# Second norm and norm statistics moved inside a chunk of a Mamba block with a quantised linear layer

## The reference

```
x = x + mamba(layernorm(x))
x = x + layernorm(x) @ W.T + bias          # W = scale * (code - 128), 1024 x 1024, blocks of 32

mamba(u): x1, z = split(u @ in_proj)       # 1024 -> 2 x 2048
          xc  = silu(conv4(x1) + conv_b)   # causal convolution over rows
          dt_r, B, C = rmsnorm(xc @ x_proj.T, ...)         # 64, 16, 16 columns
          dt  = softplus(dt_r @ dt_proj.T + dt_bias)
          h_t = exp(dt_t * A) * h_(t-1) + dt_t * B_t * xc_t    # 2048 channels x 16 states
          y   = (sum_n C_t h_t + D * xc) * silu(z)
          return y @ out_proj.T            # 2048 -> 1024
```

## Time and profile before

| | |
|---|---|
| median of 3 runs | 4703.04 us (4701.97 to 4705.4) |
| profiled execution | 4697.21 us |
| its span, first to last instruction | 4695.4 us |
| mean granted TensorE clock (1 = full) | 0.972 |
| busy: PE matmul, PE weight load | 4448.9 us (95%), 4049.0 us (86%) |
| busy: VectorE, GpSimd, ScalarE | 4160.0 us (89%), 4039.2 us (86%), 3542.4 us (75%) |

### The profile page before, as it was taken

One profiled execution on the slowest core, in us unless ns is written; L12 is line 12 of the kernel. 1 busy time (PEld: TensorE's weight loads), 2 busy tenths in 40 slices (PEclk: granted clock), 3 DMA queues, 4 the chain that ended last, 5 costly groups with the idle time before them and its releaser, 6 DMA issues.

```text
span 4695.4 us, 80181 instructions
## 1 busy us (share of the span) xinstructions
PE 4448.9 (95%) x26656; PEld 4049.0 (86%) x26656; DVE 4160.0 (89%) x5745; ACT 3542.4 (75%) x8848; POOL 4039.2 (86%) x2942
## 2 busy tenths in 40 slices
PE   7788989999999999999999999999999999999889
PEld 6567879989898998989989898998989889898779
DVE  3898989989899998989989899998989989899981
ACT  3777787877778787777877878787787777778760
POOL 0898989989898998989989898998989899899990
PEclk9889999999999999999999999999999999999999
DMA  7324243353434435343353534334353443434232
GB/s 255 130 79 161 99 159 139 114 186 133 173 129 161 145 138 175 124 178 128 123 188 123 177 137 165 137 128 173 138 180 120 145 165 129 165 127 155 90 115 94
DMA packets 160285, 678.56 MB, mean 145 GB/s; under 512 B 21120, under 2 KB 30080, under 8 KB 110720
## 3 DMA queue, kind: packets, MB, share of 16 engines
q1 hardware_dynamic: 141440, 639.88, 39.0%
q10 hardware_dynamic: 18432, 33.56, 1.9%
HBM read 618.32 MB, written 55.05 MB: 143 GB/s over the span
## 4 chain that ended last, share of the span: by engine, by line
PE 59%; DVE 20%; POOL 7%; issue 6%; ACT 5%; DMA 1%; SPq 0%; DVEq 0%; POOLq 0%; ACTq 0%
PE g L767 13%; PE gx L594 13%; PE ys L574 12%; DVE hb L1342 11%; PE ys L614 9%; PE g L689 4%; POOL dbx L486 4%; DVE hc L1290 4%; DVE gx L1238 2%; POOL half L494 2%; PE ys L604 2%; DVE bst L1218 2%; PE gx L581 2%; ACT hb L1061 1%; PE hb L853 1%
## 5 line engine op out<-in xcount | busy, mean ns | idle before, releaser
L1342 DVE TENSOR_TENSOR_SCAN hb<-hb,dbx 128x512 f32<-128x512 f32 x2048 | 2498.0, 1220 | 108.0 <-ACT hb L1061 84.4
L486 POOL TENSOR_TENSOR dbx<-dtx,bb 128x1024 f32<-128x1024 f32 x1024 | 2421.0, 2364 | 60.1 <-DVE hb L1342 34.9
L1061 ACT ACTIVATE hb<-dt,a_neg 128x256 f32<-128x256 f32 x4096 | 1789.5, 468 | 66.3
L494 POOL TENSOR_TENSOR half<-hc 128x512 f32<-128x512 f32 x1024 | 1303.1, 1273 | 135.4 <-DVE hc L1290 120.4
L1290 DVE TENSOR_TENSOR hc<-hb,cb 128x512 f32<-128x512 f32 x2048 | 1378.9, 673 | 0.0
L574 PE MATMUL ys<-half,ident 128*128 128x256 f32 x4096 | 1073.2, 389 | 133.4 <-POOL half L494 119.2
L574 PEld LDWEIGHTS ys<-half,ident 128*128 128x128 f32 x4096 | 757.2, 194 | 254.3 <-POOL half L494 151.3
L767 PEld LDWEIGHTS g<-wo,ybuf 128*128 128x128 f32 x7680 | 954.0, 198 | 20.2 <-issue 1.3
L767 PE MATMUL g<-wo,ybuf 128*128 128x128 f32 x7680 | 966.7, 281 | 0.6 <-issue 0.6
L614 PE MATMUL ys<-xnT,wz 128*128 128x256 f32 x4096 | 928.8, 380 | 1.6 <-DVE ybuf L1301 1.6
L594 PE MATMUL gx<-xnT,wx 128*128 128x256 f32 x3968 | 904.5, 381 | 4.3 <-DMA wx<-in_win 2.6
(11 more groups left out here) (105 smaller groups left out, 2766.1 us busy)
## 6 DMA issues: line engine op xcount, KB each, us to landing
wz<-in_win SPq DMA_DIRECT2D x128, 1024.0 KB, 4.8
wx<-in_win SPq DMA_DIRECT2D x124, 1024.0 KB, 4.8
wo<-in_wout SPq DMA_DIRECT2D x123, 1024.0 KB, 4.9
wf<-wf_scratch SPq DMA_DIRECT2D x113, 512.0 KB, 3.2
xc_scratch<-xcn ACTq DMA_DIRECT2D x128, 256.0 KB, 2.1
xcs<-xc_scratch SPq DMA_DIRECT2D x128, 256.0 KB, 5.0
bb<-bc_scratch SPq DMA_DIRECT2D x64, 512.0 KB, 7.5
cb<-bc_scratch SPq DMA_DIRECT2D x64, 512.0 KB, 6.7
```

The costliest lines, as they stand in the source:

```text
L486: nc.gpsimd.tensor_tensor(dbx[:, k % 2, :].rearrange("p (n t) -> p n t", n=NQ), dtx[:, S % 2, a, :].unsqueeze(1).to_broadcast([P, NQ, T]), ...
L494: nc.gpsimd.tensor_tensor(half[:, k % 4, :], hc[:, k % 2, 0:HALF], hc[:, k % 2, HALF:GW], ALU.add).then_inc(halves, 1)
L1061: ins = nc.scalar.activation(h[:, m * T:(m + 1) * T], dt[:, j % 2, a, :], ACT.Exp, scale=a_neg[:, ds((2 * j + a) * N + 2 * v + m, 1)])
L1342: nc.vector.tensor_tensor_scan(h[:], h[:], dbx[:, k % 2, w * UW:(w + 1) * UW], 0.0, ALU.mult, ALU.add).then_inc(scans, 1)
```

## The change

- The statistics of both norms are cut into single bn_stats. Those of the first norm run one in each of pairs 1 to 4 behind `add_out`, with the aggregation in pair 5 (before: all in pair 6). Of the second norm's, one runs in pair 5, one in pair 6, two and the aggregation in pair 7 (before: all in pair 7). VectorE's extra semaphore increment goes.
- In a first pair (chunks from 2 on) TensorE does the whole output block first, with group sums 0 and 1 in it, then the second norm's transposes in two banks in turn (gx, g1), then dt, group sum 3, both halves of the input projection, and z. The second transpose group waits for `add_out` of this very pair, as it writes g1. On VectorE `add_out` moves from behind product 12 to before scan 9 and the convolution taps from before scan 13 to before scan 15; on ScalarE the two rows move behind units 5 and 6 and the four evacuations behind units 7, 8, 9 and 10, and the taps behind unit 14.
- In a last pair with a first norm, ScalarE evacuates the first transposes behind unit 4 and the skip term (before: in front of unit 4) and the others a place later too; TensorE does group sum 3 before `out_proj(2)`; VectorE does `y_gate(S, 0)` two units later, behind product 11.
- In pair 6 the first norm's scale and rows run around units 9 and 10 (before: around units 14 and 15).

The hunk that drops the semaphore `aggr_go` from the list is left out here, and the indentation is cut.

```diff
@@ -715,14 +715,15 @@
         def norm2(i):
-            if not (first and st.ffn):
-                return
+            pe.wait_ge(l2_ready, after(2 * (c - 2) + i // 2 + 1))
             if i == 0:
                 pe.wait_ge(sx_act, after(xs_done))
-                pe.wait_ge(l2_ready, after(2 * (c - 1)))
-            else:
-                pe.wait_ge(l2_evac, after(4 * (c - 2) + i))
-            transposes(xrow, i, gx, l2_tr)
+            if i == 1:
+                pe.wait_ge(o_add, after(S - PAIRS + 1))
+            if i >= 2:
+                pe.wait_ge(l2_evac, after(4 * (c - 2) + i - 1))
+            transposes(xrow, i, (gx, g1)[i % 2], l2_tr)
...
@@ -788,32 +789,55 @@
         late_group(7)
-        if first and st.ffn or last and st.norm1:
+        if first and st.ffn:
+            out_proj(0)
+            x_proj()
+            out_proj(1)
+            group(0)
+            out_proj(2)
+            group(1)
+            out_proj(3)
             norm2(0)
-            norm1(0)
+            norm2(1)
+            group(2)
+            norm2(2)
+            norm2(3)
+            dt_proj()
+            group(3)
+            x_in_proj(0)
+            x_in_proj(1)
+            z_in_proj(1)
+            group(4)
+            z_in_proj(0)
+            group(5)
+            return
+        norm1(0)
+        if last and st.norm1:
             x_proj()
-            norm2(1)
             norm1(1)
             out_proj(0)
-            norm2(2)
             norm1(2)
             group(0)
-            norm2(3)
             norm1(3)
+            out_proj(1)
         else:
...
             x_proj()
-        out_proj(1)
-        if not (first and st.ffn or last and st.norm1):
+            out_proj(1)
             group(0)
...
         group(2)
-        out_proj(2)
-        group(3)
-        dt_proj()
+        if last and st.norm1:
+            group(3)
+            out_proj(2)
+            dt_proj()
+        else:
+            out_proj(2)
+            group(3)
+            dt_proj()
         out_proj(3)
...
@@ -1109,7 +1133,7 @@
                     act.wait_ge(f_mm, after(PAIRS * (c - 2)))
-                norm_evac(x2nT, 4 * (c - 2), i, gx, l2_tr, l2_evac)
+                norm_evac(x2nT, 4 * (c - 2), i, (gx, g1)[i % 2], l2_tr, l2_evac)
...
@@ -1149,45 +1173,48 @@
         unit(1)
+        unit(2)
         norm2_start()
-        norm2_row(0)
-        unit(2)
-        norm2_row(1)
         unit(3)
...
         silus()
-        norm2(0)
-        norm1(0)
         unit(4)
         first_skip_term()
-        norm2(1)
+        norm1(0)
+        unit(5)
+        norm2_row(0)
         norm1(1)
-        unit(5)
-        norm2(2)
+        unit(6)
+        norm2_row(1)
         norm1(2)
-        unit(6)
-        norm2(3)
+        unit(7)
+        norm2(0)
         norm1(3)
-        unit(7)
         rms_square()
         unit(8)
+        norm2(1)
         rms_apply()
+        norm1_start()
         unit(9)
+        norm2(2)
+        norm1_row(0)
         unit(10)
+        norm2(3)
+        norm1_row(1)
         unit(11)
...
         unit(12)
-        x_taps()
+        if not (first and st.ffn):
+            x_taps()
         dt_softplus()
...
         unit(14)
-        norm1_start()
-        norm1_row(0)
+        if first and st.ffn:
+            x_taps()
         unit(15)
-        norm1_row(1)
...
@@ -1212,20 +1239,26 @@
         def _(dve):
-def stats(rows, bst, mv, mid, done, n):
-    for tt in range(TT):
-        for h in range(2):
-            ins = nc.vector.bn_stats(bst[:, tt, 6 * h:6 * h + 6], rows(tt, h))
-    ins.then_inc(mid, 1)
-    dve.wait_ge(mid, after(n))
-    dve.sem_inc(aggr_go, 1)
+def aggregate(bst, mv, mid, done, n):
+    dve.wait_ge(mid, after(4 * n))
     for tt in range(TT):
...
+def norm1_piece(chunk, i):
+    tt, h = divmod(i, 2)
+    dve.wait_ge(xrow_in, landed(chunk + 1))
+    dve.wait_ge(l1_stats, after(chunk))
+    nc.vector.bn_stats(bst1[:, tt, 6 * h:6 * h + 6], xrow[:, tt, h * 512:(h + 1) * 512]).then_inc(l1_dve, 1)
+def norm1_aggregate(chunk):
+    aggregate(bst1, mv1, l1_dve, l1_stats, chunk + 1)
 def norm1_stats(chunk):
-    dve.wait_ge(xrow_in, landed(chunk + 1))
-    stats(lambda tt, h: xrow[:, tt, h * 512:(h + 1) * 512], bst1, mv1, l1_dve, l1_stats, chunk + 1)
+    for i in range(4):
+        norm1_piece(chunk, i)
+    norm1_aggregate(chunk)
...
@@ -1272,11 +1305,15 @@
-def norm2_stats_of(chunk):
-    dve.wait_ge(o_add, after(PAIRS * (chunk + 1)))
-    rows = x2[:, chunk % 2, :]
-    stats(lambda tt, h: rows[:, tt * H + h * 512:tt * H + (h + 1) * 512], bst2, mv2, l2_dve,
-          l2_stats, chunk + 1)
+def norm2_piece(chunk, tt, h):
+    dve.wait_ge(o_add, after(PAIRS * chunk + 4 * (h + 1)))
+    dve.wait_ge(l2_stats, after(chunk))
+    nc.vector.bn_stats(bst2[:, tt, 6 * h:6 * h + 6],
+                       x2_rows(chunk % 2)[:, tt, h * 512:(h + 1) * 512]).then_inc(l2_dve, 1)
+def norm2_aggregate(chunk):
+    aggregate(bst2, mv2, l2_dve, l2_stats, chunk + 1)
...
@@ -1385,9 +1422,18 @@
-        def norm2_stats():
-            if last and st.outproj:
-                norm2_stats_of(c - 1)
+        def norm_stats():
+            if st.norm1 and 1 <= j <= 4:
+                norm1_piece(c + 2, j - 1)
+            if st.norm1 and j == 5:
+                norm1_aggregate(c + 2)
+            if st.outproj and j in (5, 6):
+                norm2_piece(c - 1, j - 5, 0)
+            if st.outproj and last:
+                norm2_piece(c - 1, 0, 1)
+                norm2_piece(c - 1, 1, 1)
+                norm2_aggregate(c - 1)
...
@@ -1413,24 +1459,31 @@
         product(7)
+        if first and st.ffn:
+            add_out()
         scan(9)
         product(8)
-        if pre and st.norm1:
-            norm1_stats(c + 2)
         scan(10)
         product(9)
-        y_gate(S, 0)
+        if not (last and st.norm1):
+            y_gate(S, 0)
         scan(11)
...
         product(11)
-        taps()
+        if last and st.norm1:
+            y_gate(S, 0)
+        if not (first and st.ffn):
+            taps()
         scan(13)
         product(12)
-        add_out()
-        norm2_stats()
+        if not (first and st.ffn):
+            add_out()
+        norm_stats()
         scan(14)
         product(13)
+        if first and st.ffn:
+            taps()
         scan(15)
...
@@ -1455,7 +1508,10 @@
     block_add(NC - 1, j, hb[j % 2], o_add)
-norm2_stats_of(NC - 1)
+for tt in range(TT):
+    for h in range(2):
+        norm2_piece(NC - 1, tt, h)
+norm2_aggregate(NC - 1)
 for j in range(1, PAIRS):
...
 for j in range(PAIRS):
```

More of the change, by code:

```diff
@@ L215, in build_program @@
         xp_add, o_add, f_add = sem("xp_add"), sem("o_add"), sem("f_add")
-        rms_red, l1_dve, l1_stats, l2_dve, l2_stats, aggr_go = (sem("rms_red"), sem("l1_dve"), sem("l1_stats"),
-                                                                sem("l2_dve"), sem("l2_stats"), sem("aggr_go"))
+        rms_red, l1_dve, l1_stats, l2_dve, l2_stats = (sem("rms_red"), sem("l1_dve"), sem("l1_stats"),
+                                                                sem("l2_dve"), sem("l2_stats"))
         deq_a, deq_b, a_ready = sem("deq_a"), sem("deq_b"), sem("a_ready")
```

## The result

The changed kernel takes **4738.62 us** (median of 4 runs, 4732.54 to 4744.98); beside it the kernel before took 4702.51 (4701.74 to 4705.4). The ratio is 1.0076, with 95% between 1.0058 and 1.0093: 36 us slower. I had forecast 4705, from 4676 to 4734, so the result is outside the range, on its slow side. The profiled execution took 4737.06 us, its span is 4735.2 us and its mean granted clock 0.973, where before it was 4697.21, 4695.4 and 0.972. The two spans differ by 39.8 us, and that is what has to be found.

The account below looks back on a forecast made before the run. TensorE was taken to fill the middle pairs, so only first and last pairs counted: -1.4 us for 14 chunks and +3 for statistics made +2, 4699 in the profiled execution and 4705 as median, range 4676 to 4734.

Parts of the forecast that it names:

- so this hides: Pairs 1 to 6: VectorE's 1.44 us wait at the gating covers the added statistics; pairs stay at 33.20, cost 0.
- Chunks 0 and 1: Statistics in pieces cost 2 to 3 us once in chunk 1, 0 to 2 in chunk 0; +3 in all.
- The last pair: Last pair: 0.5 us gained before group 7, 1.35 lost waiting for the first evacuation; 38.5, 0.85 longer.
- The first pair: First pair: waits for half sums and silu go, TensorE idles 0.95 and 3.85 us; 42.1, 0.95 shorter.
- rival D: First pair: x lands at 21.5, `add_out` waits 1.5 us; 21 more in all, 4726; chance 0.08.
- The clock: First pair: the single 3.85 us wait brings a fall to half clock, costing 2.0 us.
- rival B: First pair: TensorE's single pause brings no clock fall, or one under a microsecond; 28 us less, 4677; chance 0.24.
- rival C: Last pair: the clock falls there as well, behind the wait for the first evacuation; 28 us more, 4733; chance 0.20.
- For 14 chunks: Sum over the loop: +0.85 - 0.95 = -0.1 us per chunk, for 14 chunks -1.4.
- F: First pair: `add_out` comes at 17, VectorE not held by unit 8; 68 us less, 4637; chance 0.04.

Follow-up runs that it names:

- with gx: The changed kernel with all four groups of the second norm's transposes in gx, so none waits for `add_out`: 4681.54 us, ratio 0.9959.
- with unit 8 first: The changed kernel with ScalarE's unit 8 in front of the evacuation of the second norm's first transposes: 4731.53 us, ratio 1.0062.
- with the unread matmuls: The changed kernel with nine matmuls nobody reads between the second norm's first and second transposes, in chunks 2 to 14: 4718.5 us, ratio 1.0038.

## Why the prediction was wrong, and where it was right

Three steps failed. The idle time at the gating was taken to cover the statistics ("so this hides", 0); it does not, and they cost 0.65 us in a chunk, 8.0 in all. The chain to TensorE's second transposes in a first pair was right in kind and too short: TensorE starts again at 21.7 us and not at 20.5, and this is most of the 15.6 us that these pairs are off in all. And the first pairs of chunks 2 and 15 were given a gain of 0.95 each, and lost 7.7 us together.

**The statistics' middle pairs: wrong step.** "It stands 1.44 us at the gating in every middle pair, so this hides" took the wait of an instruction ahead of the addition as its cover. The pieces stand behind the gating, in front of the last products, and what follows from those is POOL's half sum 7 and TensorE's group 7. The room there was smaller. In the kernel before, that half sum started 2.52 us into pair 3 and now starts 3.10 into it; the 0.58 that it is later used up the room and left a wait of 0.23, and a pair 0.10 longer. A bn_stats is 0.62, so the room was about 0.5, and the aggregation's pair passes it further, 0.25 in pair 6. The run with the pieces in front of the gating shows it from the other side: 33.20 everywhere. That is 0.65 in a chunk, 8 us in twelve.

**Chunks 0 and 1: right within the scatter.** I had +3, and two last pairs at 0.85, in all 4.7. At the start of chunk 2's first pair the changed kernel is 7.4 us behind (685.47 against 678.10). But the kernels with gx, with unit 8 first and with the unread matmuls have the same instructions up to there, and are 4.0, 6.2 and 5.5 behind. So one execution can't tell the 7.4 from my 4.7. With the statistics alone it is 3.2 (681.31), for the +3; with the pieces in front of the gating 2.9 ahead (675.23), so here too it is their place that costs.

**The last pair: right.** 38.40 against my 38.5; the second transposes wait 1.58 (I had 1.7), scan 13 waits 2.56 (2.3), VectorE's wait at the gating is gone. The kernel with the evacuations in their old places gives 1.41 for that term (1.35).

**The first pair: the mechanism right, its size too small.** I had TensorE start again 20.5 us into the pair, and it does at 21.74 (16.87 up to the first transposes, 4.87 from there to the second, means of ten). That is the whole miss: 43.32 - 42.1 = 1.22, and 21.74 - 20.5 = 1.24. All behind the restart takes 21.58 where I had 21.6, in which 0.3 less for the clock is made up by 0.3 more elsewhere, which I did not find row by row. The 1.24 has two parts.
- 0.66 before the first transposes. `out_proj(0)` starts at 6.78 on average and not at 6.42, and groups 0 and 1 stretch once more. POOL runs late there: in the pair shown the chain runs through it from the landing of B rows at 2931.84 to group 1 at 2951.49, and two small additions into bb and a wait of 1.44 for the B rows stand in its list. I had looked at VectorE and ScalarE in this stretch, and not at POOL.
- 0.58 between the two. My chain of copy, unit 8, scan 8, product and `add_out` was right in its links and 0.35 short in their sum, and in some chunks x from memory adds up to 0.7. I had x issued at 13.6, 9.3 us behind its store as before; it was 15.5, since x was issued 11.2 behind the store now. So half of rival D's reason held. The waits for `add_out` run from 4.04 to 4.73, where I had 3.85.

The clock I had at 2.0. It costs 1.70 behind the restart, and 2.06 was got back by keeping TensorE busy. That a pause of four microseconds brings a fall (rival B's question) was right. On this the Trainium skill, in "TensorE: Matmul & The Clock Gate", section "Why this matters for your kernels", advises against idle gaps as long as one idle window between bursts. The trace agrees for the wait of 4.04 us. For last pairs that section says less than the runs: in the kernel with gx waits of 0.72 and 1.56 us, with work between them, were followed by a fall in one chunk, and waits of 0.73 and 1.57 in the next by none. So rival C's mechanism is real here at a price of about 1.6 us, though no last pair of the changed kernel shows it.

**"For 14 chunks": wrong at the edges.** I gave the first pairs of chunks 2 and 15 the same gain of 0.95 as the others. They had no such loss to give. Chunk 2's took 38.10 before and takes 42.78, chunk 15's took 35.18 and takes 38.22. In chunk 2's the wait for half sums of 2.7 us stands in both kernels, and that of 4.04 for `add_out` takes the place of 1.65 for the silu. That is 4.68 + 3.04 = 7.7 us to the bad, where I had 1.9 to the good; two windows of the kernel before would have told me.

Sum of the misses: 8.0 for the middle pairs of twelve chunks; 15.6 for the first pairs of chunks 3 to 14 (43.36 on average after 43.00, 0.35 longer each where I had 0.95 shorter); 9.6 for the two edges; 2.7 for chunks 0 and 1, inside their scatter; 3.4 for the other pairs of chunks 14 and 15, which I had left out; and 1.0 back for the last pairs. That is 38.3, for the 38.2 between my +1.6 and the 39.8 found. (In the prediction 33.20 + 4 x 0.44 is 34.96 and not 34.98, which changes nothing.) The remark that what the change wins at the start of a first pair goes into a new wait in its middle held. It was five terms on the same side, three of them at the ends of the loop, and the prediction had put the error of its offsets at about 0.7 us in a chunk.

**The rivals.** B and F did not come. D decided in six of thirteen first pairs, by 0.2 to 0.7 us and not by 1.5, and is the next limit. C needed another timing. What was missing was a rival in which several small terms add up, with the edges of the loop counted one by one.

## What to carry to other kernels

A wait covers only what stands in front of it on its engine. Work put behind it must fit into the room of the next thing downstream, so find that release (here half sum 7 to group 7, about 0.5 us) before calling an instruction free, and put it in front of the wait instead: the same bn_stats cost 0.1 us behind and nothing in front. A second bank that frees a transpose from one wait may tie it to a longer one; follow that new wait around all engines to see whether it comes back to the engine that waits. When one repair moves a wait by less than it should, look for a second limit right beside it, and try the repairs together.

## What the runs showed of the hardware

- The same idle time need not have the same result for the clock: last pairs with waits of 0.72 and 1.56 us fell to half clock in six of twelve chunks and stayed at full clock in the others, in one execution, and in the changed kernel, with 0.70 and 1.58, in none of twelve. The fall shown has 3.3 us at clock 0.50 and made its pair 1.6 longer; over the six, 1.4 to 2.8.
- The statistics alone gave first pairs that alternate, 40.78 and 41.87, with equal waits; their mean clock was 0.96 and 0.92:

```profile
3182.74:3223.52 40.78, 37.07 (x221) 33.63 (x220) 33.38 (x46) 32.26 (x79) 33.76 (x27) 0.96 0.69 259
2904.02:2945.89 41.87, 38.17 (x222) 34.72 (x220) 33.38 (x46) 32.27 (x79) 33.73 (x27) 0.92 0.67 251
```

- A bn_stats of 512 columns takes 0.68 us alone, and 2.47 for four in a row.
- x, issued at 2943.76 with xcs and wf right behind it, let `add_out` go at 2948.73: 5.0 us, as long as the 4.9 before.
